# Cross attention's output: split in rows by head pairs and turned by DMA, in place of TensorE's transposes

## The reference

```python
x = layernorm(x + self_attention(x))            # 16 heads, relative positions, over the 8 rows of T
# cross attention, per one of 8 batches of 512 queries and 512 keys, 8 heads of 64
q = (x @ W_tgt.T + b_tgt) * mask;  k, v = split((ctx @ W_src.T + b_src) * mask)
o = softmax(q k.T / 8, masked keys -inf) v      # 512 x 512: 8 heads side by side
x = layernorm(x + concat(x, o) @ W_out.T + b_out)
# feed forward, 512 -> 2048 -> 512, hidden and second weight in fp8 (e4m3)
x = layernorm(x + fp16(fp8(relu(x @ w1.T + b1)) @ fp8(w2).T + b2))
```

## Time and profile before

| | us |
|---|---|
| median of 3 runs | 1878.28 |
| lowest, highest | 1867.21, 1881.26 |
| profiled execution, its own time | 1870.93 |
| its span, first to last instruction | 1869.1 |
| TensorE busy | 1775.7 (95%) |
| VectorE busy | 1374.0 (74%) |
| ScalarE busy | 770.5 (41%) |
| GpSimd busy | 566.8 (30%) |
| mean granted TensorE clock | 0.987 |

### The profile page before, as it was taken

The page is one execution under the profiler, slowest core; times in us unless marked ns, Lnnn a source line. Parts: engine busy times, 40 slices in busy tenths (PEclk is TensorE's granted clock), DMA queues, the critical chain, the costliest instruction groups (busy, mean ns, idle before and its releaser), DMA issues. The chain is left out here.

```text
span 1869.1 us, 32453 instructions
## 1 busy us (share of the span) xinstructions
PE 1775.7 (95%) x12432; PEld 978.3 (52%) x12432; DVE 1374.0 (74%) x1466; ACT 770.5 (41%) x1208; POOL 566.8 (30%) x578
## 2 busy tenths in 40 slices
PE   7999999999999998978899999999999999999988
PEld 3665456545654564634545555455454554554543
DVE  2899999999999999957566577575675666657721
ACT  3323222222232222237657265373562744726522
POOL 3125865596559525600100302003011020030000
PEclk9999999999999999999999999999999999999999
DMA  9436346535653467556430613405205143051010
GB/s 217 128 74 136 97 124 153 130 79 137 148 123 85 118 143 184 156 147 201 103 74 2 142 46 74 113 1 130 57 14 134 40 106 81 1 137 28 13 34 23
DMA packets 295166, 183.86 MB, mean 98 GB/s; under 512 B 194015, under 2 KB 251359, under 8 KB 295038
## 3 DMA queue, kind: packets, MB, share of 16 engines
q1 hardware_dynamic: 287392, 178.50, 38.3%
q10 hardware_dynamic: 7646, 3.50, 1.0%
HBM read 94.82 MB, written 33.62 MB: 69 GB/s over the span
## 5 line engine op out<-in xcount | busy, mean ns | idle before, releaser
L1223 POOL TENSOR_TENSOR q<-q,x_hi 128x512 f16<-128x512 f32 x28 | 40.5, 1475 | 597.5 <-ACT x_hi L1571 597.5
L1251 PE MATMUL b_ff<-x2T_hi,w1T_hi 128*128 128x512 f16 x512 | 195.3, 381 | 2.3 <-DVE x2T_lo L1661 2.3
L1251 PE MATMUL b_ff<-x2T_lo,w1T_hi 128*128 128x512 f16 x512 | 195.3, 381 | 0.0
L1251 PE MATMUL b_ff<-x2T_hi,w1T_lo 128*128 128x512 f16 x512 | 195.1, 381 | 0.0
L1661 DVE TENSOR_TENSOR p_lo<-k,p_hi 128x1024 f16<-128x1024 f32 x128 | 161.3, 1260 | 37.4 <-ACT p_hi L1517 37.4
L1550 ACT ACTIVATE k<-b_st,mbias 128x512 f32<-128x512 f32 x256 | 161.9, 693 | 41.4 <-PE b_st L1318 37.9
L1711 DVE SCALAR_TENSOR_TENSOR top<-b_st,mleast,top 128x512 f16<-128x512 f32 x168 | 126.1, 751 | 51.5 <-PE b_st L1278 34.5
L825 DVE TENSOR_TENSOR prod<-q,k 128x4096 f32<-128x4096 f32 x32 | 143.0, 4469 | 20.7 <-ACT q L691 19.9
L607 PE MATMUL sm_b<-cT_hi,wsT_hi 128*128 128x256 f16 x512 | 141.1, 276 | 14.7 <-DMA cT_lo<-rows_lo 12.2
L457 POOL TENSOR_TENSOR rows_lo<-cn,rows_hi 128x512 f16<-128x512 f32 x64 | 131.4, 2061 | 61.0 <-ACT rows_hi L675 61.0
L571 PE MATMUL pj_b<-winT_hi,xT_hi 128*128 128x512 f16 x384 | 148.1, 386 | 0.9 <-DVE winT_lo L892 0.9
(11 more groups left out here) (287 smaller groups left out, 4314.1 us busy)
## 6 DMA issues: line engine op xcount, KB each, us to landing
cn<-in_ctx_dram SPq DMA_DIRECT2D x64, 256.0 KB, 3.3
k<-kT_scratch SPq DMA_DIRECT2D x24, 512.0 KB, 7.9
x<-in_x_dram SPq DMA_DIRECT2D x32, 256.0 KB, 3.1
x_scratch<-x SPq DMA_DIRECT2D x32, 256.0 KB, 2.3
q<-x_scratch SPq DMA_DIRECT2D x8, 1024.0 KB, 5.6
q<-x_scratch SPq DMA_DIRECT2D x32, 256.0 KB, 2.8
out_dram<-q SPq DMA_DIRECT2D x32, 256.0 KB, 3.3
xn<-in_x_dram SPq DMA_DIRECT2D x24, 256.0 KB, 2.9
```

Source lines behind the costliest of these rows:

```text
L1251: mm = pe.matmul(out, a, c, start=(start and n == 0), stop=end)
```

## The change

The attention output o is no longer one array with the rows' tiles side by side but four arrays `o[j]`, one for each pair of heads. When both heads of pair j are normalized, ScalarE copies the pair's 128x512 values to float16 (`o_rows_high`, into the new `o_hi[j]`), GpSimd subtracts to get the low halves (`o_rows_lo`, into the front of `o[j]` itself), and SyncE issues two DMA transposes (`turn_o`) into oT_hi and oT_lo. Pairs 0 to 2 are split during the heads (after heads 3, 5 and 7 on ScalarE), pair 3 at the end, on ScalarE after `normalize` of output tiles 0 and 1, on GpSimd after their factors. TensorE's 16 transposes, the four evictions on ScalarE and the four on VectorE are gone, in each of the 8 batches. `output_rest` waits for all eight DMA transposes (`o_turned`). The first head of the next batch waits for them as well before it writes `o[0]` and `o_hi[0]`.

On SyncE, turns of pairs 0 to 2 stand ahead of `load_heads` of the next batch, and pair 3's turn stands after the stores of tiles 0 and 1. The stores of tiles 2 and 3 and the residual rows 0 and 1 now stand ahead of x1's turn of tile 0, residual rows 2 and 3 ahead of x1's turns 1 to 3. After batch 0's heads the turns of pairs 2 and 3 both stand ahead of `load_heads(1)` and of x1's turns. In batch 0 `output_x1` tile 0 stays ahead of `values` of head 7, and tiles 1 to 3 go behind it.

```diff
+            def turn_o(b, j):
+                sp.wait_ge(s["o_row_lo"], 4 * b + j + 1)
+                stand_alone(sp, alone["sp"])
+                for dst, rows in ((oT[0], o_hi[j][:, :]), (oT[1], o_lo[j])):
+                    sp.dma_start_transpose(dst[:, j, :].rearrange("p (t c) -> p t c", t=4), rows).then_inc(
+                        s["o_turned"], 16)
...
             for n in range(4, FT):
                 load_weights(n)
+                if n in (11, 15):
+                    turn_o(0, n // 4 - 2)
+            turn_o(0, 2)
+            turn_o(0, 3)
             load_heads(1, False)
             for tt in range(4):
                 turn_x1(1, tt)
...
                 load_x1(b + 2)
+                for j in range(3):
+                    turn_o(b + 1, j)
                 load_heads(b + 2, False)
-                for half in ((0, 1), (2, 3)):
-                    for tt in half:
-                        store(b, tt)
-                    for tt in half:
-                        turn_x1(b + 2, tt)
-                    for tt in half:
-                        load_residual(b + 1, tt, False)
+                for tt in range(4):
+                    store(b, tt)
+                    if tt == 1:
+                        turn_o(b + 1, 3)
+                for tt in (0, 1):
+                    load_residual(b + 1, tt, False)
+                turn_x1(b + 2, 0)
+                for tt in (2, 3):
+                    load_residual(b + 1, tt, False)
+                for tt in range(1, 4):
+                    turn_x1(b + 2, tt)
...
+            def o_rows_lo(b, j):
+                pool.wait_ge(s["o_row_hi"], 4 * b + j + 1)
+                stand_alone(pool, alone["act"])
+                pool.tensor_tensor(o_lo[j], o[j], o_hi[j][:, :], ALU.subtract).then_inc(s["o_row_lo"], 1)
+
+            for j in range(3):
+                o_rows_lo(0, j)
             for tt in range(4):
                 x1_rows_lo(1, tt)
+            o_rows_lo(0, 3)
             with pool.Fori(0, NBATCH - 2) as b:
                 for tt in range(4):
                     norm_factors("l2", b, tt)
+                for j in range(3):
+                    o_rows_lo(b + 1, j)
                 for tt in range(4):
                     x1_rows_lo(b + 2, tt)
                 for tt in range(4):
                     norm_factors("l3", b, tt)
+                    if tt == 1:
+                        o_rows_lo(b + 1, 3)
...
                 feed_forward2(ff, 2)
                 feed_forward2(ff, 3)
-                pe.wait_ge(s["o_norm"], 8 * b + 8)
-                for tt in range(4):
-                    transposes(tq_b[tt], o[:, tt, :], s["ot_filled"])
                 output_x1(ff)
...
-                output_x1(None)
+                output_x1(None, (0,))
                 values(0, H2 - 1)
-                pe.wait_ge(s["o_norm"], 8)
-                for tt in range(4):
-                    transposes(tq_b[tt], o[:, tt, :], s["ot_filled"])
+                output_x1(None, (1, 2, 3))
 
             def output_rest(b):
-                pe.wait_ge(s["ot_lo"], 4 * b + 4)
+                pe.wait_ge(s["o_turned"], 128 * b + 128)
...
+            def o_rows_high(b, j):
+
+                act.wait_ge(s["o_norm"], 8 * b + 2 * j + 2)
+                stand_alone(act, alone["act"])
+                if j == 0 and not (isinstance(b, int) and b == 0):
+                    act.wait_ge(s["o_turned"], 128 * b)
+                    stand_alone(act, alone["act"])
+                act.activation(o_hi[j][:, :], o[j], ACT.Copy).then_inc(s["o_row_hi"], 1)
...
                     if h + 1 < H2:
                         relu(ff, 2 * h + 2)
                         maximum_row(b, h + 1)
+                    if h in (3, 5, 7):
+                        o_rows_high(b, (h - 3) // 2)
                 if rows:
                     x1_rows_high(b + 1, False)
                 normalize("l3", ff, 0)
                 normalize("l3", ff, 1)
-                for tt in range(4):
-                    hi(col(oT[0], tt), bank4(tq_b[tt]), s["ot_filled"], 4 * b + tt + 1, s["ot_hi"])
+                o_rows_high(b, 3)
                 normalize("l3", ff, 2)
                 normalize("l3", ff, 3)
```

More of the change, by code:

```diff
@@ L1030, in phase_b @@
     x1n, x2 = w.x1n, w.q[:, 4:8, :]
-    o, pf = w.k[:, 0:4, :], w.k[:, 4:8, :]
+    o, pf = [w.k[:, j, :] for j in range(KT)], w.k[:, 4:8, :]
+    o_hi, o_lo = [sb(f"o_hi{j}", [P, B], F16) for j in range(KT)], [z.bitcast(F16)[:, 0:B] for z in o]
     x1T = pair("x1T", [P, KT, B])
@@ L1073, in phase_b @@
              "negm", "mr_filled", "mr_copied", "st_filled", "st_exp", "p_hi", "p_lo", "av_filled", "o_rden",
-             "o_norm", "x1_row_hi", "x1_row_lo", "x1_used", "ot_filled", "ot_hi", "ot_lo", "om_filled", "om_used", "x2t_filled", "x2t_hi", "x2t_lo",
+             "o_norm", "x1_row_hi", "x1_row_lo", "x1_used", "o_row_hi", "o_row_lo", "o_turned", "om_filled", "om_used", "x2t_filled", "x2t_hi", "x2t_lo",
              "f1_filled", "relu", "f2_filled", "f2_used", "f2_sum", "l2_stats", "l2_mv", "l2_rstd", "l2_done",
@@ L1200, in _ @@
                 queries(last, g)
+            for j in range(3):
+                turn_o(last, j)
             for tt in range(4):
                 store(last - 1, tt)
+                if tt == 1:
+                    turn_o(last, 3)
             for tt in range(4):
@@ L1233, in _ @@
                     norm_factors("l3", b, tt)
+                    if tt == 1:
+                        o_rows_lo(b + 1, 3)
             last = NBATCH - 1
             for at in (last - 1, last):
-                for l in ("l2", "l3"):
-                    for tt in range(4):
-                        norm_factors(l, at, tt)
+                for tt in range(4):
+                    norm_factors("l2", at, tt)
+                for j in range(3) if at != last else ():
+                    o_rows_lo(last, j)
+                for tt in range(4):
+                    norm_factors("l3", at, tt)
+                    if tt == 1 and at != last:
+                        o_rows_lo(last, 3)
         @block.tensor
@@ L1362, in feed_forward2, with output_x1 @@
                          None, s["f2_filled"])
-            def output_x1(ff):
-                for tt in range(4):
+            def output_x1(ff, tiles=range(4)):
+                for tt in tiles:
                     if tt >= 2:
@@ L1481, in queries_and_first_scores @@
                 x2_transposes(ff)
+                pe.wait_ge(s["o_norm"], 8 * b)
                 queries(b, 3, slice(None, 8))
@@ L1613, in first_heads @@
                         weights_high(2 * h + 2)
+                    if h in (3, 5, 7):
+                        o_rows_high(0, (h - 3) // 2)
                 x1_rows_high(1, True)
-                for tt in range(4):
-                    hi(col(oT[0], tt), bank4(tq_b[tt]), s["ot_filled"], tt + 1, s["ot_hi"])
+                o_rows_high(0, 3)
             def x2_hi(b):
@@ L1742, in normalized @@
                 dve.wait_ge(s["o_rden"], 8 * b + h + 1)
-                dve.tensor_tensor(o[:, :, h * D2:(h + 1) * D2], av[:, :, 0:D2],
+                if h == 0 and not (isinstance(b, int) and b == 0):
+                    dve.wait_ge(s["o_turned"], 128 * b)
+                    stand_alone(dve, alone["dve"])
+                dve.tensor_tensor(o[h // 2].rearrange("p (t c) -> p t c", t=4)[:, :, h % 2 * D2:(h % 2 + 1) * D2],
+                                  av[:, :, 0:D2],
                                   rden[:, h % 2, :].unsqueeze(2).to_broadcast([P, 4, D2]),
@@ L1776, in heads @@
                 feed_forward_sum(ff, 3)
-                for tt in range(4):
-                    low(col(oT[1], tt), bank4(tq_b[tt]), col(oT[0], tt), s["ot_hi"], 4 * b + tt + 1, s["ot_lo"])
             def first_heads():
@@ L1794, in first_heads @@
                 normalized(0, H2 - 1)
-                for tt in range(4):
-                    low(col(oT[1], tt), bank4(tq_b[tt]), col(oT[0], tt), s["ot_hi"], tt + 1, s["ot_lo"])
             def first_queries_and_maximum():
```

1 line of the change is left out of this document (removed).

## The result

| | before | after |
|---|---|---|
| median, us (20 runs each) | 1874.76 | 1884.74 |
| lowest, highest | 1867.21, 1881.26 (one of 4250 stands apart) | 1878.97, 1891.22 |
| span of the profiled execution | 1869.1 | 1879.9 |
| mean granted clock | 0.987 | 0.984 |

What follows compares the result with a forecast made beforehand. TensorE's own list was taken as the bound, with only 4.0 us of waiting in 827. The terms -11.1 - 0.5 + 4.2 + 1.75 made it 5.65 us slower, forecast 1880 us, range 1864 to 1895.

Steps and rivals of the forecast that it cites:

- batch 0's end, delay: After batch 0's heads, the next queries start 8.6 us later (8.1 to 9.1), waiting for x1's turns.
- batch 0's end, half clock: After TensorE's 10 us pause behind batch 0, 4 to 6 us at half speed, 2.5 us lost.
- batch 0's heads: Splitting o beside batch 0's heads, with VectorE fuller there, costs 0.5 us, bounds 0 and 2.7.
- six full batches: Ends of batches 1 to 6: each gains 0.2 to 1.3 us, taken as 0.7, together 4.2.
- batch 7: After the last batch nothing stands ahead of pair 3's turn, so the full 1.75 us is gained.
- After batch 0: Loads start at 927.75, 9.8 us later; queries at about 950.2; with half clock, batch 0's end costs 11.1 us.
- Inside the heads: ScalarE's copies hide in its idle time; the split costs nothing in full batches and 0.5 us in batch 0.
- rival of a slowed VectorE: GpSimd's low halves delay VectorE's maxima in the heads: 19 us at most, 10 likely, total 1890; chance 0.06.
- Pair 3 in a full batch: Pair 3's turns land F+10.2 to F+11.4 (F: former transposes' start), wanted at F+10.36: wait 0 to 1.0 us.
- x1's turns in a full batch: Last turn lands by F+23.1 (F: former transposes' start), queries start F+22.0 to F+23.1; 0.7 us gained a batch.
- The queue binding each batch: Rival: SyncE's blocked issues delay x1's last turn to F+27, 3.7 us lost a batch, 32 slower; chance 0.10.
- TensorE's 14 us nearly whole: Rival: issue never blocks and batch 0's end costs less, so 3.5 us faster, 1866 to 1875; chance 0.18.

Runs made afterwards that it cites:

- e3: Changed kernel, but in each full batch the next values are loaded behind x1's turns: 1872.43 us, 0.9998 of the kernel before.
- e5: Changed kernel with batch 1's keys and values loaded behind x1's turns, and each full batch's next values too: 1858.42 us, 0.9929 of the kernel before.
- e2: Changed kernel, but after batch 0 the keys and values of batch 1 are loaded behind x1's turns: 1874.92 us, 1.0013 of the kernel before.
- e1: Changed kernel, but batch 0 as before, its o transposed by TensorE without split or turns: 1874.77 us, 1.0011 of the kernel before.
- e6: Changed kernel with batch 0 as before, and in full batches the next values loaded behind x1's turns: 1861.34 us, 0.9940 of the kernel before.
- e7: Kernel before, with only the next values loaded behind x1's turns and the residual rows: 1873.32 us, 1.0000 of the kernel before.
- e8: Changed kernel, but x1's turn of tile 0 ahead of residual rows 0 and 1 in full batches: 1876.16 us, 1.0022 of the kernel before.
- e4: Changed kernel, but full batches' stores, x1's turns and residual rows in the old halves, pair 3's turn behind store 1: 1882.92 us, 1.0059 of the kernel before.
- e9: Changed kernel, but in full batches pair 2's turn is issued behind the next keys and values: 1888.43 us, 1.0082 of the kernel before.

## Why the prediction was right or wrong

It said 1880, range 1864 to 1895, and no change to be told or slightly slower: 1884.74 was measured. The size was off by nearly half: 5.65 us slower were forecast, 10.0 were measured by the medians and 10.8 by the traces, and the range is wide enough to hold that. The terms, by the trace:

| term | predicted | measured |
|---|---|---|
| batch 0's end, delay | -8.6 | -8.5 |
| batch 0's end, half clock | -2.5 (2 to 3) | -1.4 |
| batch 0's heads | -0.5 (0 to 2.7) | -1.5, not of the split, else open |
| six full batches | +4.2 (1.2 to 7.8) | **-2.1** |
| batch 7 | +1.75 | +1.75, and 0.9 of clock, not of the change |
| sum | -5.65 | -10.8 |

**Which view bounds the kernel: right.** TensorE's list, its waits and its clock account for the whole difference, and e3 and e5 give 1.75 in each full batch when nothing else is late. In batch 0 they don't: the forecast had the 1.75 inside its -8.6, and in e5 new waits take it back.

**After batch 0: right.** Forecast were loads at 927.75, x1 turned at 949.8 to 950.8 and the queries at 950.2; it was 928.84, 951.6 and 951.69, with 1.5 of the delay from earlier in the phase. e2 shows that the order does it: with the loads behind the turns the wait is 0.58. The clock fell to 0.50 as in the earlier trace rows, but for 3 us and not 4 to 6, so 1.4 was lost.

**Inside the heads: right for the full batches.** The rival of a slowed VectorE is dead: e3's batch is before's less 1.75 to a hundredth. Batch 0's 1.5 was not a price of the split. From TensorE's first transposes of the phase to the end of the 0.60 us wait for `p_lo` it took 90.7 us before and 92.1 after. e1 and e6, which have no split in batch 0, took 92.4 and 91.5, and the kernels with it 91.4 to 92.6. e7, with before's own lists there, took 90.0. The clock has a part in it: in the windows 840 to 844 and 844 to 848 it was 0.73 and 0.50 after, and 0.78 and 0.79 before. Whether it is that alone stays open. The two kernels that keep o in one array are the two shortest, and no run tells whether the new layout has a part in that.

**Pair 3 in a full batch: right.** Forecast F+10.2 to F+11.4; `output_rest` started between F+10.36 and F+11.03, a wait of 0 to 0.5 after it. The landings in the order of issue, on which this stood, held: store 1, issued at 1052.4, landed 9.0 later at 1061.4, and pair 3's turns landed at 1052.91 + 9.0 = 1061.9 and 1055.73 + 6.7 = 1062.4, 0.5 apart each. Eight blocks took 1.0 us behind the store. The Trainium skill ("VectorE: DVE Perf Modes", The three transpose paths) gives 1309 ns for 128x128 through the crossbar, by which eight would take 10.5, an estimate. After batch 0 four blocks needed 2.5 us from issue to landing, with no loads left ahead of them in the queue; by that figure they would need 5.2, an estimate too. The measurement decides.

**x1's turns in a full batch: this step failed.** It forecast queries between F+22.0 and F+23.1, 0.7 us gained a batch. They started at F+23.5 to F+23.9. The sum "Unblocked, pair 3 is issued by F+4.7, the rest needs 6 x 0.65 + 4 x 2.76 = 14.9" holds the issue times only and no wait of SyncE. But residual row 0 waits until store 0 has landed. The store's landing had been used one paragraph earlier, for pair 3, and the description of the kernel says of the residual rows that each "waits until the store of that tile has landed"; the two were not put together. Store 0 needed 10.8 us here against 8.5 to 9.5 in the earlier trace rows, and SyncE stood still for 1.3 us with all of x1's turns behind. The end of pair 3's held-up turns was forecast at F+6.5 and was F+6.8. The rest of the list took 14.3 us without the pause, where 14.9 were forecast. So the last turn landed 0.3 + 1.3 - 0.6 = 1.0 us behind the F+22.6 that I took, at F+23.6. e8 shows the pause's part: with tile 0 ahead of the residuals, 1.3 us a batch come back. e3 shows both parts together.

**The rivals.** The queue binding each batch: its mechanism was the right one, its size not. Its point was F+23.3 for the last landing, and the last landing came at F+23.6; priced at F+27 it would have cost 3.7 a batch, it cost 0.35. The 0.10 was too little for the mechanism; as the way to slower by over 1% it was fair. TensorE's 14 us nearly whole: not in this kernel, but with the order mended e5 comes near it. Of its 13.5 us, 12.3 are transposes (seven batches), the rest is clock and the start of the phase.

**"Residual rows 2 and 3 come 5 us earlier, but TensorE never waited for them"** was true of before and no reason: e4 shows that they are next in line as soon as the old order is put behind blocked turns.

## What to carry to other kernels

When work moves from an engine to a DMA, write down the issuing engine's whole list with its waits, not only its issue times: an issue can stand still for a landing or behind bulk loads, and everything urgent behind it pays. Bulk loads that nobody needs for a long time belong behind the small transfers that somebody waits for next; the same edit is worth 0 before the change and 2.1 us a batch after it. Work taken off an engine is only a gain where nothing else becomes the last to be late: the same 1.75 us counted in full in seven batches and not at all in batch 0. And when a wait is taken away by reordering, look at what the moved item feeds, as with the residual rows, since it will be the next to be late.

## What the runs showed of the hardware

An issue of a DMA transpose on SyncE takes 1.2 to 1.3 us when nothing is in its way. Behind the heads' loads, some 2.8 MB, it took longer, and the sooner it came the longer: 5.55 us when begun 5.2 us behind the first load's issue (e9), 4.56 at 5.7 us (after batch 0), and 2.78 at 8.9 us (pair 3, with two stores between).

The same turn of four blocks lands 2.4 to 2.5 us after its issue with no loads left ahead of it, and later behind them: pair 3's turns needed 6.7 to 9.0.

TensorE's clock fell to half after pauses much shorter than the 5.9 us that the prediction went by, but not each time. In the kernel after it stayed full over the 4 us behind each of the six waits of 1.47 to 1.86 us. Among the longer ones, the length doesn't sort them. It stayed at 1.00 behind 2.21 us in e2 and behind 2.24, 2.33 and 2.44 in e9. It was 0.57 over the 4 us behind 2.04 in e1, and 0.62, 0.66 and 0.59 behind 2.48, 3.09 and 3.63 in e9. Windows of e1 and e9 that hold two of these:

```profile
1556.00:1560.00 4.00, 3.43 (x10) 1.33 (x11) 0.18 (x1) 0.00 (x0) 1.12 (x4) 0.64 0.00 0
...
1204.00:1208.00 4.00, 3.99 (x13) 1.62 (x14) 0.00 (x0) 0.00 (x0) 0.14 (x1) 0.67 0.00 0
```

What decides it no run here shows. In e1 the batch with that pause took 124.92, the other five 121.8 to 122.4. Its wait for x1 was 0.2 to 0.5 longer than theirs, and its wait for pair 3 was 0.7; the low clock behind them cost about 1.7, worked out from 0.57 over 4 us. So a wait for a DMA near 2 us can cost more than its own length. Without that batch e1's mean is 122.04, which is why its 122.52 in the table is no worse than after's 122.25.
